# A delta-rule scan whose DRAM tensors are laid out by chunk of 64 tokens, with its small packing transfers joined and its decays loaded in halves

## The chip, the cores and the metric

The kernel runs on one core of a Trainium2 chip. A core has five engines that run side by side and meet only at semaphores: TensorE (PE in the rows, with its weight loads as PEld), VectorE (DVE), ScalarE (ACT), GpSimd (POOL) and SyncE (SP). Here SyncE issues every transfer between DRAM and the core's memory (SBUF), in one queue, in the order of its program; 16 DMA engines carry them out. The metric is device time of one execution, in microseconds (us).

## The reference

Everything is float32. The program is one hybrid decoder block; six of its stages touch what is changed here. Cut to what they compute, for H = 16 heads of 128 and T = 2048 tokens:

```
q, k, v = (silu(dwconv_causal(x @ W.T, taps of 4)) for each W in Wq, Wk, Wv); k *= 128 ** -0.5
a    = sigmoid(x @ Wa.T + ba)         # a decay for each head and value dimension
beta = sigmoid(x @ Wb.T + bb)         # one number for each head
def step(St, inp):                    # St is (head, 128, 128), over 2048 tokens
    err = einsum('bhij,bhj->bhi', St, kt) - vt
    Sn  = at[..., None] * St - (bt[..., None] * err)[..., None] * kt[:, :, None, :]
    ot  = einsum('bhij,bhj->bhi', Sn, qt)
out = layernorm_per_head(o) * sigmoid(x @ Wg.T) @ Wo.T + x
```

Behind it stand a feed-forward layer, a sparse attention and a second feed-forward layer; the change leaves them alone.

## The kernel before, in words

The stages run one after another, each with its own buffers and semaphores and a barrier behind it.

**project_phase** computes, head by head, five streams (beta_k, q, k, beta_v and a, the decay) as 128 x 2048 tiles and stores each as one megabyte in DRAM, laid out (head, partition, token): one run of 8 KB on each partition. SyncE stores them in `stores`, and behind them loads the row of beta and the weights of the head after next.

**gram_phase** loads keys, beta_k and q of one head (three transfers of 1 MB, two heads in flight), multiplies keys with themselves and with q in windows of 144 tokens, and stores the products near the diagonal in `band` (8 transfers of 64 KB a head) and the transposed keys in `kT` (8 transfers of 128 KB a head).

**scan_phase** is the recurrence. It goes through 128 blocks of C = 16 tokens, all 16 heads at once. Four blocks (BPC) make a chunk of 64 tokens, two chunks a turn (RING = 128 tokens, 8 blocks); `v` is a block's place in its chunk. Three kinds of work are prepared chunk by chunk: SyncE packs dot products out of `band` into `dots` (`pack_dots`), loads them to all partitions (`load_dots`, 2.5 MB), copies bands into two zero-padded DRAM buffers `xz` and `uz` (`build`, 24 transfers a chunk) and loads those (`load_grams`); ScalarE negates some dots (`negate`, in block v = 0); GpSimd makes out of dots and decays the small triangular matrices of the next chunk (`prepare`, 33 operations and more, a chunk ahead).

In each block VectorE runs four steps (`solve(0)` to `solve(3)`). Each but the last hands its result to TensorE to be turned (L1519), ScalarE copies it (L1402), TensorE applies it to the rest of the block (L1529), and the next `solve` begins with L1677. Among these steps VectorE multiplies the four quarters of the state by the block's decays, `decay_state(0)` in the middle of the block, (1) later, (2) and (3) at its end (L1733). Before the first quarter it waits for `abar`, the decays of this block spread to all partitions, 1 MB in one buffer:

```
dve.wait_ge(abar_in, 16 * (b + 1))          # decay_state(0)
sp.wait_ge(s_decayed, 4 * (b + 1))          # SyncE: all four quarters done,
load_abar(b + 1)                            # then the next block's decays
```

SyncE's queue in a chunk, in order: v = 0 loads keys and grams of the next chunk and abar; v = 1 packs the dots of a chunk of the next turn (28 transfers) and loads abar; v = 2 builds (24 transfers) and loads abar; v = 3 loads k and q, abar, then, once GpSimd has finished `prepare` (`pre_done`), the decays `avec` and the dots `gram` for GpSimd's next chunk, and v. The stores of the output stand in v = 1 and v = 3. `avec` and `gram` have one buffer each.

Two operations of VectorE in a block take both of their inputs from SBUF: `carry_first` (L1700, in the first third of a block) and the scaling of UB (L1750, in its middle). GpSimd's `prepare` works in SBUF alone.

**mix_phase** loads the scan's output `o` head by head (L547, 64 transfers of 256 KB), norms and gates it and multiplies by Wo.

## Time and profile before

| | us |
|---|---|
| median of 3 runs | 9192.23 (9132.13 to 9202.69) |
| the profiled execution | 9095.78, span 9094.0 |
| projections | 207 to 1072 |
| gram stage | 1120 to 1415 |
| scan, from the first to the last decay of a state quarter | 1504.3 to 4344.2 |
| mix stage | 4388 to 4975 |

The span is the time from the first to the last instruction of the profiled execution. That execution is one run; the median above is of three others and lies 1.05% higher. A group of rows below is one answer of the trace. "Idle before" is the time in which an engine stood still before an instruction, with the instruction or transfer that released it. SPq is SyncE's queue: the duration of a row there is that of issuing, not of the transfer.

### The profile page before, as it was taken

The page shows a single profiled execution, that of the slowest core. Times are in us where ns is not written, and L with a number is a line of the kernel's source. Part 1 is how long each engine was busy: PE and PEld are TensorE (multiplying, and loading weights), DVE is VectorE, ACT ScalarE, POOL GpSimd, SP SyncE. Part 2 cuts the span into 40 slices and gives each one's busy share as a digit, 9 for nine tenths or more (in the row PEclk, how much of TensorE's full clock was granted, in tenths as well). Part 3 has the DMA queues.
Part 4 walks back from the last instruction along what each step waited for, and adds up shares of the span by engine and source line. Part 5 has one row for each costly group of instructions (what it writes and reads, how often), then busy time and mean ns, then how long its engine had stood idle before and what let it go on. Part 6 is the DMA issues. An engine that isn't in the chain of part 4 may idle for free. (4 is left out here: it accounts for less than half of the span.)

```text
span 9094.0 us, 86277 instructions
## 1 busy us (share of the span) xinstructions
PE 6326.3 (70%) x24276; PEld 3976.1 (44%) x24276; DVE 5051.7 (56%) x7260; ACT 2599.2 (29%) x4821; POOL 2080.9 (23%) x1465
## 2 busy tenths in 40 slices
PE   2888663555555555565697996955435989989799
PEld 1766542333333333333354784422224842222487
DVE  3888712656756666666566332277887743333332
ACT  1322221232223223232343211144431223333121
POOL 0554404445454535453010110100000000000011
PEclk6999875555555555555799997966555568888899
DMA  4333485545454444444212003211102211110200
GB/s 145 135 136 130 153 261 139 154 124 147 115 156 137 136 138 136 140 132 123 100 55 68 28 21 113 78 45 35 28 15 45 56 42 38 28 37 20 101 28 26
DMA packets 960301, 850.70 MB, mean 94 GB/s; under 512 B 656944, under 2 KB 834736, under 8 KB 907952
## 3 DMA queue, kind: packets, MB, share of 16 engines
q1 hardware_dynamic: 960032, 847.89, 31.9%
q14 instruction: 195, 1.60, 0.1%
q8 instruction: 74, 1.21, 0.1%
HBM read 655.85 MB, written 198.63 MB: 94 GB/s over the span
## 5 line engine op out<-in xcount | busy, mean ns | idle before, releaser
L888 POOL TENSOR_TENSOR ffn_hid_low<-ffn_hid,ffn_hid_high 128x512 fp32r<-128x512 f32 x128 | 164.9, 1288 | 3581.3 <-ACT ffn_hid_high L878 3581.3
L298 PE MATMUL proj_acc<-proj_xn,proj_w 128*128 128x512 f32 x3072 | 729.1, 400 | 125.0 <-ACT proj_decay L344 90.8
L1529 PE MATMUL scan_pq<-scan_inner,scan_uT 64*128 64x128 f32 (+1 forms) x768 | 341.9, 545 | 599.2 <-ACT scan_uT L1402 416.5
L2351 PE MATMUL attend_ot<-attend_e,attend_v 128*64 128x512 f32 (+3 forms) x1280 | 693.4, 632 | 90.2 <-ACT attend_e L2378 90.2
L298 PEld LDWEIGHTS proj_acc<-proj_xn,proj_w 128*128 128x128 f32 x3072 | 594.3, 194 | 259.8 <-ACT proj_decay L344 93.8
L391 DVE SCALAR_TENSOR_TENSOR proj_y<-proj_raw,proj_cw,proj_y 128x2048 f32<-128x2048 f32 x144 | 574.5, 3990 | 19.1 <-DVE proj_y L387 2.7
L1519 PE MATMUL scan_turn<-scan_idt,scan_ud 128*128 128x128 f32 x384 | 172.2, 449 | 573.9 <-DVE scan_ud L1689 552.2
L1975 PE MATMUL csum_sc<-csum_qk 96*128 96x512 f32 (+3 forms) x640 | 289.6, 569 | 395.6 <-ACT csum_e L1999 350.2
L1733 DVE TENSOR_TENSOR scan_S<-scan_S,scan_abar 128x512 f32<-128x512 f32 x508 | 339.3, 691 | 313.6 <-DMA scan_abar<-decays 313.3
L1529 PEld LDWEIGHTS scan_pq<-scan_inner,scan_uT 64*128 64x128 f32 (+1 forms) x768 | 182.7, 295 | 717.0 <-ACT scan_uT L1402 509.3
L1677 DVE TENSOR_TENSOR scan_pq<-scan_pq,scan_reach 128x48 f32<-128x48 f32 x512 | 108.8, 212 | 688.7 <-PE scan_pq L1529 624.3
L941 DVE TENSOR_TENSOR ffn_hid<-ffn_gate,ffn_l 128x512 f32<-128x512 f32 x128 | 88.0, 687 | 583.0 <-PE ffn_l L824 352.2
L2019 DVE TENSOR_REDUCE csum_mx<-csum_sc 128x1 f32<-128x2048 f32 (+15 forms) x256 | 327.4, 1284 | 143.9 <-PE csum_sc L1978 143.9
L2410 DVE SCALAR_TENSOR_TENSOR attend_sc<-attend_far,attend_hcol,attend_sc 128x128 f32<-128x128 f32 x464 | 141.4, 348 | 474.4 <-PE attend_sc L2340 382.2
L2236 DVE TENSOR_REDUCE cmax_peak<-cmax_sc 128x1664 f32 (+22 forms) x256 | 328.1, 1291 | 116.1 <-PE cmax_sc L2197 113.8
L1519 PEld LDWEIGHTS scan_turn<-scan_idt,scan_ud 128*128 128x128 f32 x384 | 67.1, 175 | 739.9 <-DVE scan_ud L1689 433.3
L1483 PE MATMUL scan_S<-scan_UTm,scan_kT 32*128 32x256 f32 x2032 | 385.0, 675 | 0.0
L824 PE MATMUL ffn_g<-ffn_xn,ffn_w 128*128 128x512 f32 x1536 | 372.6, 392 | 10.4 <-issue 10.4
L824 PE MATMUL ffn_l<-ffn_xn,ffn_w 128*128 128x512 f32 x1536 | 369.0, 389 | 0.0
L1975 PEld LDWEIGHTS csum_sc<-csum_qk 96*128 96x128 f32 x640 | 156.9, 279 | 482.1 <-ACT csum_e L1999 408.0
L2340 PEld LDWEIGHTS attend_sc<-attend_qk 98*128 98x128 f32 x640 | 132.7, 207 | 525.4 <-issue 284.3
L2378 ACT ACTIVATE attend_e<-attend_sc,attend_hcol 128x512 f32<-128x512 f32 (+3 forms) x448 | 271.2, 605 | 258.7 <-PE attend_sc L2340 256.5
(230 smaller groups left out, 14390.7 us busy)
## 6 DMA issues: line engine op xcount, KB each, us to landing
scan_abar<-decays SPq DMA_DIRECT2D x128, 1024.0 KB, 5.2
scan_gram<-dots SPq DMA_DIRECT2D x32, 2560.0 KB, 13.4
scan_cross<-xz SPq DMA_DIRECT2D x128, 256.0 KB, 5.0
scan_inner<-uz SPq DMA_DIRECT2D x32, 1024.0 KB, 7.5
csum_qk<-qk SPq DMA_DIRECT2D x96, 256.0 KB
cmax_qk<-qk SPq DMA_DIRECT2D x96, 256.0 KB
attend_qk<-qk SPq DMA_DIRECT2D x96, 256.0 KB
proj_beta_rows<-beta SPq DMA_DIRECT2D x16, 1024.0 KB, 8.2
```

The source lines that it names most:

```text
L298: mm = pe.matmul(acc[:, (j * TT + t) % 8, :], w[:, u, wh, j, k, :], xn[:, xh, k, t * TOK:(t + 1) * TOK], start=(p == 0 and k == 0), stop=( ...
L391: dve.scalar_tensor_tensor(y[:, s % 2, :], src, cwt, y[:, s % 2, :], ALU.mult, ALU.add).then_inc(conv_step, 1)
L824: mm = pe.matmul(ps[:, x % 2, :], w[:, u, wh, k, n * P:(n + 1) * P], xn[:, xh, k, t * TOK:(t + 1) * TOK], start=(a == 0 and k == 0), stop= ...
L1483: mm = pe.matmul(S[:, q, g].rearrange("p e i -> p (e i)"), keys[32 * q:32 * q + 32, g, :], UTm[32 * q:32 * q + 32, g].rearrange("p e i -> ...
L1519: pe.transpose(turn_ps[:, 0:P], ud[:, slot:slot + 2].rearrange("p j h s -> p (j h s)"), idt[:, :]).then_inc(ut_done, 1)
L1529: pe.matmul(pq[:, u % 2].rearrange("p h w t -> p (h w) t")[:, :, t0:t0 + n], uT[0:k, :], inner[0:k, half, v, :, t1:t2], start=False, stop= ...
L1733: dve.tensor_tensor(S[:, q], S[:, q], abar[:, q], ALU.mult).then_inc(s_decayed, 1)
L1975: pe.matmul(sc[:, n % 2, c:c + w], qk[:, u, 0, q * P:(q + 1) * P], qk[:, u, 1, c:c + w], start=True, stop=(c + w < (q + 1) * P))
L2019: dve.tensor_reduce(mx[:, n % 2:n % 2 + 1], sc[:, n % 2, 0:(q + 1) * P], AX.X, ALU.max, negate=True).then_inc(maxed, 1)
L2236: dve.tensor_reduce(peak[:, bass.ds(h * NT + q, 1)], sc[:, n % 2, 0:(q + 1) * P], AX.X, ALU.max, negate=True).then_inc(peaked, 1)
L2351: pe.matmul(ot[:, g % 2, lo:TOK], v[:, u, kt, :], e[:, x % RINGS, lo:TOK], start=(kt == 0), stop=(x == last_of[g])).then_inc(summed, 1)
L2378: op = act.activation(e[:, x % RINGS, near:TOK], sc[:, x % RINGS, near:TOK], ACT.Exp, bias=hcol[:, u, kt:kt + 1], scale=SCALE)
```

## The change

The streams, the transposed keys, the padded buffers and the output are laid out in DRAM so that what the scan loads for a chunk lies in one run on each partition: streams as (chunk, partition, head, 64 tokens), `kT` as (chunk, half, partition, 4 blocks x 128), `xz` and `uz` with the four blocks of a chunk side by side, `o` as (32 tokens, partition, head, 32). What writes the streams (projections) and what reads them head by head (gram stage, mix stage) now moves pieces: 256 bytes each for the streams, 128 bytes for `o`.

The rows of `band` are shifted by their block's place in the chunk (row length ROW = 112 instead of 64), so that the 16 units of a chunk lie at even distances: `pack_dots` needs 7 transfers of 256 pieces instead of 28 of 64. `abar` is loaded in two halves with a semaphore each; the first half is asked for once two quarters of the state are done. `build` is cut by block and spread over v = 1 (one), v = 2 (two), v = 3 (one). `avec` and `gram` are loaded at v = 2 instead of v = 3. In the prologue the packing stands ahead of the loads of k and q.

```diff
-    streams = [scratch(f"stream_{n}", (H, P, T)) ...]
+    streams = [scratch(f"stream_{n}", (T // CHUNK, P, H, CHUNK)) ...]
-    band = scratch("band", (H, GH, C, T // P, 2, 2 * C))
-    kT = scratch("kT", (2 * T // C, P, P))
-    xz = scratch("xz", (2, BPC, 2, P * 256 + 256))
-    uz = scratch("uz", (2, BPC, P, 512))
+    band = scratch("band", (H, GH, C, T // P, ROW))
+    kT = scratch("kT", (T // CHUNK, 2, P, BPC * P))
+    xz = scratch("xz", (2, 2, P * BPC * 2 * GH * C + GH * 2 * C))
+    uz = scratch("uz", (2, P, BPC * 2 * H * C))
-    o = scratch("o", (H, P, T))
+    o = scratch("o", (T // (2 * C), P, H, 2 * C))
...
             def pack_dots(it, half):
-                for v in range(BPC):
-                    at0 = band[:, BPC * half + v, 0, bass.ds(it, 1), 0]
-                    for q, row in ((1, 0), (1, 1), (1, 2), (1, 3), (0, 0), (0, 1), (0, 2)):
...
-                        rows = bass.AP(band.tensor, at0.offset + row * TROW + q * C + first, [[HROW, H], [4 * TROW + 4, 4], [1, n]])
+                at0 = band[:, BPC * half, 0, bass.ds(it, 1), 0]
+                for q, row in ((1, 0), (1, 1), (1, 2), (1, 3), (0, 0), (0, 1), (0, 2)):
...
+                    rows = bass.AP(band.tensor, at0.offset + row * TROW + q * C + first, [[HROW, H], [4 * TROW + 4, SPC], [1, n]])
...
-            def load_abar(b):
-                sp.dma_start(abar[:, :, :, :, :]..., decays[bass.ds(b, 1), :].to_broadcast([P, H * P])).then_inc(abar_in, 16)
+            def load_abar(b, part):
+                sp.dma_start(abar[:, 2 * part:2 * part + 2]..., decays[..., part * H * P // 2:(part + 1) * H * P // 2]...).then_inc(abar_in[part], 16)
...
-                    if u % BPC == 2 and more:
-                        sp.wait_ge(grams_in[half], 16 * 5 * (it + 1))
-                        build(it + 1, half)
+                    if v == 1 and more:
+                        sp.wait_ge(grams_in[half], 16 * 2 * (it + 1))
+                        build(it + 1, half, 0)
+                    if v == 2 and more:
+                        build(it + 1, half, 1)
+                        build(it + 1, half, 2)
+                    if v == 3 and more:
+                        build(it + 1, half, 3)
                     if more or u < BPR - 1:
+                        sp.wait_ge(s_decayed, 4 * b + 2)
+                        load_abar(b + 1, 0)
                         sp.wait_ge(s_decayed, 4 * (b + 1))
-                        load_abar(b + 1)
-                    if u % BPC == BPC - 1 and more:
+                        load_abar(b + 1, 1)
+                    if v == 2 and more:
                         sp.wait_ge(pre_done, 2 * it + half + 2)
                         load_a(it + 1, half)
                         load_dots(it + 1, half)
...
                 def decay_state(q):
-                    if q == 0:
-                        dve.wait_ge(abar_in, 16 * (b + 1))
+                    if q % 2 == 0:
+                        dve.wait_ge(abar_in[q // 2], 16 * (b + 1))
```

How SyncE's queue moves, in two places. The names are target<-source, then the shape; a row that ends in x2 stands for two such transfers.

SyncE, end of block v = 2 and block v = 3 in the first turn, before:

```order
L1296 DMA scan_abar<-decays 128x2048
L1234 DMA scan_ring<-stream_beta_k 128x16x64
L1234 DMA scan_ring<-stream_q 128x16x64
L1296 DMA scan_abar<-decays 128x2048
L1243 DMA scan_avec<-stream_a 128x16x64
L1261 DMA scan_gram<-dots 128x5120
L1292 DMA o<-scan_oring 128x16x32
```

and with the change:

```order
L1300 DMA scan_abar<-decays 128x1024 x2
L1251 DMA scan_avec<-stream_a 128x1024
L1267 DMA scan_gram<-dots 128x5120
L1244 DMA scan_ring<-stream_beta_k 128x1024
L1244 DMA scan_ring<-stream_q 128x1024
L1273 DMA xz<-band 16x16x32
L1277 DMA uz<-band 16x4x12
L1279 DMA uz<-band 16x4x4
L1277 DMA uz<-band 16x4x12
L1279 DMA uz<-band 16x4x4
L1281 DMA uz<-band 16x4x32
L1300 DMA scan_abar<-decays 128x1024 x2
```

`avec` and `gram` stood behind the second abar of this stretch, at the end of block v = 3, and now stand behind the abar of v = 2, a block earlier; six transfers of a build lie between k, q and the next abar.

SyncE, block v = 1 in the first turn, with the change, from the abar ahead of it on (before, the same place had 28 rows `dots<-band 16x4x4` to `16x4x1` and no build):

```order
L1300 DMA scan_abar<-decays 128x1024 x2
L1263 DMA dots<-band 256x1x4
L1263 DMA dots<-band 256x1x3
L1263 DMA dots<-band 256x1x2
L1263 DMA dots<-band 256x1x1
L1263 DMA dots<-band 256x1x3
L1263 DMA dots<-band 256x1x2
L1263 DMA dots<-band 256x1x1
L1273 DMA xz<-band 16x16x32
L1277 DMA uz<-band 16x4x12
L1279 DMA uz<-band 16x4x4
L1277 DMA uz<-band 16x4x12
```

The packing is 7 transfers with 256 rows each where it was 28 with 64; one build of six transfers follows, of which four show here, and then the two halves of abar.

## Rows read from the trace of the kernel before

**Rows 1.** Stages: stretch, us, busy of PE, PEld, DVE, ACT, POOL; clock, DMA share, GB/s.

```profile
207.00:1072.00 865.00, 729.05 (x3072) 594.31 (x3072) 731.00 (x237) 252.13 (x319) 432.99 (x107) 0.93 0.37 132
1120.00:1415.00 295.00, 190.86 (x768) 145.64 (x768) 58.58 (x128) 86.29 (x192) 0.00 (x0) 0.79 0.88 261
1504.30:4344.20 2839.90, 1598.57 (x8491) 945.54 (x8493) 1819.65 (x4052) 830.55 (x1766) 1300.07 (x1085) 0.54 0.48 135
4388.00:4975.00 587.00, 520.19 (x1536) 294.37 (x1536) 358.61 (x272) 234.93 (x247) 66.64 (x64) 0.95 0.18 58
```

**Rows 2.** Waits in the scan, 1440 to 4370: us in total, times, longest us.

```profile
DVE scan_pq L1677 <- PE scan_pq L1529: 624.3, 305, 33.7
...
ACT scan_gram L1361 <- DMA scan_gram<-dots: 398.1, 32, 49.7
...
DVE scan_S L1733 <- DMA scan_abar<-decays: 313.3, 65, 8.8
```

**Rows 3.** SyncE in order of time over one chunk: start us, us to issue.

```profile
2627.88 21.27 SPq L1257 DMA_DIRECT2D dots<-band  x28
2649.42 0.36 SPq L1296 DMA_DIRECT2D scan_abar<-decays  x1
...
2663.25 0.55 SPq L1268 DMA_DIRECT2D xz<-band  x1
...
2672.59 0.36 SPq L1296 DMA_DIRECT2D scan_abar<-decays  x1
...
2673.68 4.21 SPq L1234 DMA_DIRECT2D scan_ring<-stream_q  x1
...
2688.61 4.04 SPq L1261 DMA_DIRECT2D scan_gram<-dots  x1
```

**Rows 4.** VectorE in order of time over the same chunk; in brackets the idle time.

```profile
2655.06 0.70 DVE L1733 TENSOR_TENSOR scan_S<-scan_S,scan_abar 128x512 f32<-128x512 f32 x1 [6.36 <-DMA scan_abar<-decays]
...
2678.05 0.70 DVE L1733 TENSOR_TENSOR scan_S<-scan_S,scan_abar 128x512 f32<-128x512 f32 x1 [8.82 <-DMA scan_abar<-decays]
...
2705.07 0.22 DVE L1677 TENSOR_TENSOR scan_pq<-scan_pq,scan_reach 128x48 f32<-128x48 f32 x1 [11.28 <-PE scan_pq L1529]
...
2711.15 1.49 DVE L1722 TENSOR_REDUCE scan_oring<-scan_oprod 128x256 f32<-128x1280 f32 x1
...
2719.53 0.69 DVE L1733 TENSOR_TENSOR scan_S<-scan_S,scan_abar 128x512 f32<-128x512 f32 x1
...
2724.38 0.69 DVE L1733 TENSOR_TENSOR scan_S<-scan_S,scan_abar 128x512 f32<-128x512 f32 x1
...
2728.36 1.49 DVE L1722 TENSOR_REDUCE scan_oring<-scan_oprod 128x256 f32<-128x1280 f32 x1
```

**Rows 5.** The start of the scan, GpSimd and VectorE in order of time.

```profile
1465.02 1.80 POOL L1559 TENSOR_TENSOR scan_gram<-scan_avec,scan_gram 128x512 f32<-128x512 f32 x1 [15.44 <-ACT scan_gram L1361]
...
1538.68 0.22 DVE L1677 TENSOR_TENSOR scan_pq<-scan_pq,scan_reach 128x48 f32<-128x48 f32 x1 [33.67 <-PE scan_pq L1529]
```

**Rows 6.** VectorE beside GpSimd: one stretch, then groups (busy us, mean ns, idle).

```profile
2084.63 15.66 DVE L1750 TENSOR_TENSOR scan_UB<-scan_ud,scan_suffix 128x192 f32<-128x192 f32 x1
...
2085.24 2.99 POOL L1562 TENSOR_TENSOR scan_Mhat<-scan_Mhat,scan_gram 128x768 f32<-128x768 f32 x1
...
2099.11 0.97 POOL L1562 TENSOR_TENSOR scan_Mhat<-scan_Mhat,scan_tmp 128x256 f32<-128x256 f32 x1
...
L1750 DVE TENSOR_TENSOR scan_UB<-scan_ud,scan_suffix 128x192 f32<-128x192 f32 x127 | 192.8, 1518 | 0.0
...
L1700 DVE TENSOR_TENSOR scan_ud<-scan_ud,scan_reach 128x64 f32<-128x64 f32 x128 | 111.5, 871 | 0.0
```

**Rows 7.** Columns of rows 1: 8 KB pieces loading (gram stage), 256-byte pieces (scan).

```profile
1154.00:1158.00 4.00, 0.00 (x0) 0.00 (x0) 0.00 (x0) 0.00 (x0) 0.00 (x0) 0.50 1.02 406
2678.00:2681.00 3.00, 0.51 (x2) 0.24 (x2) 2.85 (x9) 0.28 (x1) 0.00 (x0) 0.50 1.25 223
```

**Rows 8.** Waits of ScalarE in the projections, 207 to 1072.

```profile
ACT proj_w L310 <- DMA proj_ab<-in_ba: 48.9, 14, 4.7
```

More of the change, by code:

```diff
@@ L960 @@
 DOTS = 20
+ROW = 4 * C + CHUNK - C
 def gram_phase(nc, streams, band, kT_dram, padded, ident, T):
@@ L995, in load @@
             def load(h, u):
-                one = lambda s: streams[s][bass.ds(h, 1)].rearrange("o p t -> p (o t)")
-                sp.dma_start(keys[:, u, :], one(KK)).then_inc(k_in[u], 16)
-                sp.dma_start(both[:, u, 0, 0:T], one(KB)).then_inc(both_in[u], 16)
-                sp.dma_start(both[:, u, 1, 0:T], one(QQ)).then_inc(both_in[u], 16)
+                one = lambda s: streams[s][:, :, bass.ds(h, 1)].rearrange("c p o t -> p c (o t)")
+                pieces = lambda x: x.rearrange("p (c t) -> p c t", t=CHUNK)
+                sp.dma_start(pieces(keys[:, u, :]), one(KK)).then_inc(k_in[u], 16)
+                sp.dma_start(pieces(both[:, u, 0, 0:T]), one(KB)).then_inc(both_in[u], 16)
+                sp.dma_start(pieces(both[:, u, 1, 0:T]), one(QQ)).then_inc(both_in[u], 16)
             def store(i, u):
@@ L1243, in load_a @@
                 sp.dma_start(avec[:, :, :, :].rearrange("p h n s -> p h (n s)"),
-                             streams[3][:, :, bass.ds(it * RING + half * CHUNK, CHUNK)]
-                             .rearrange("h p t -> p h t")).then_inc(a_in, 16)
+                             streams[3][bass.ds(2 * it + half, 1)].rearrange("o p h t -> p (o h) t")).then_inc(a_in, 16)
             def pack_dots(it, half):
-                for v in range(BPC):
-                    at0 = band[:, BPC * half + v, 0, bass.ds(it, 1), 0]
-                    for q, row in ((1, 0), (1, 1), (1, 2), (1, 3), (0, 0), (0, 1), (0, 2)):
-                        first = row + 1 - q
-                        n = 4 - first
-                        place = 4 * row if q else 13 + 3 * row
-                        rows = bass.AP(band.tensor, at0.offset + row * TROW + q * C + first, [[HROW, H], [4 * TROW + 4, 4], [1, n]])
-                        out = bass.AP(dots.tensor, half * DOTS * U + (4 * v) * DOTS + place, [[SPC * DOTS, H], [DOTS, 4], [1, n]])
-                        sp.dma_start(out, rows, allow_slow_non_contiguous=n == 1).then_inc(packed[half], 16)
+                at0 = band[:, BPC * half, 0, bass.ds(it, 1), 0]
@@ new lines, in pack_dots @@
+                for q, row in ((1, 0), (1, 1), (1, 2), (1, 3), (0, 0), (0, 1), (0, 2)):
+                    first = row + 1 - q
+                    n = 4 - first
+                    place = 4 * row if q else 13 + 3 * row
+                    rows = bass.AP(band.tensor, at0.offset + row * TROW + q * C + first, [[HROW, H], [4 * TROW + 4, SPC], [1, n]])
+                    out = bass.AP(dots.tensor, half * DOTS * U + place, [[SPC * DOTS, H], [DOTS, SPC], [1, n]])
+                    sp.dma_start(out, rows, allow_slow_non_contiguous=n == 1).then_inc(packed[half], 16)
@@ L1298, in _ @@
             load_a(0, 0)
-            load_kq(0, 0)
             pack_dots(0, 0)
             load_dots(0, 0)
-            build(0, 0)
+            load_kq(0, 0)
+            for v in range(BPC):
+                build(0, 0, v)
             load_keys(0, 0)
@@ L1305, in _ @@
             load(RV, 0, 0, vb_in[0])
-            load_abar(0)
+            for part in range(2):
+                load_abar(0, part)
             load_kq(0, 1)
@@ L1309, in _ @@
             pack_dots(0, 1)
-            build(0, 1)
+            for v in range(BPC):
+                build(0, 1, v)
             sp.wait_ge(pre_done, 1)
@@ L1344, in turn @@
                         store(it, u)
-                    if u % BPC == BPC - 1:
-                        if more:
-                            sp.wait_ge(r_done, NSUB * (b + 1))
-                            load(RV, it + 1, half, vb_in[half])
+                    if v == BPC - 1 and more:
+                        sp.wait_ge(r_done, NSUB * (b + 1))
+                        load(RV, it + 1, half, vb_in[half])
             turn(0, True)
```

107 lines of the change are left out of this document (55 added, 52 removed).

## The prediction

> **What bounds the kernel.** I read first the busy time by stage [rows 1]. The change touches four stages. In the scan, 2840 us for 127 blocks or 22.4 us a block, no engine is full: VectorE is busy 64%, TensorE 56% at a granted clock of 0.54 of full, near the lower of its two levels (1.2 of 2.4 GHz), the DMA engines 48%. So the scan is a chain of short steps through VectorE, TensorE and ScalarE, and what counts is what holds that chain. The gram stage is the opposite: the DMA engines are busy 88% at 261 GB/s. In the projections VectorE leads (85%) and DMA has room (37%); in the mix stage TensorE leads and DMA is at 18%.
>
> Then the waits of the scan [rows 2]. VectorE waits 313.3 us for `abar` in 65 places, and 624.3 us before L1677, for the step that TensorE and ScalarE give back. Most of the latter is the chain itself; the part that can go is that ScalarE waits 398.1 us for the dots `gram` before `negate`, and the copy that VectorE needs next stands behind it in ScalarE's program.
>
> Then one chunk in order of time [rows 3, 4]. Packing takes SyncE 21.27 us, building the 23.2 us from 2649.42 to 2672.59, and each has an abar behind it that could have gone earlier; VectorE stands 6.36 and 8.82 us. `avec` and `gram` go out at the very end of the chunk, and in the next block VectorE stands 11.28 us. That is 26.5 us of 89.5 a chunk. A block with none of this, from one reduction of the output to the next, takes 17.2 us (2711.15 to 2728.36).
>
> Last, VectorE beside GpSimd [rows 6]. The two operations with both inputs in SBUF are sometimes held: L1750 took 15.66 us, until GpSimd's run of instructions was over (2099.11 + 0.97). Against the 0.35 and 0.22 us that they take unheld, they lose 127 x 1.17 + 128 x 0.65 = 232 us, 7.5 us a chunk. The change leaves GpSimd's work as it is.
>
> **The sum**, against the profiled execution (9095.8 us).
>
> *The waits for abar.* Seven packing transfers take, at the 0.74 us from one small transfer to the next (a piece-rich one of 256 rows, xz, issues in 0.55 us too [rows 3]), about 5.3 us, and the build between them 4.5. In the clean block the first quarter is decayed 8.4 us and the second, done, 13.9 us after the reduction before [rows 4]. So the first half of abar may be asked for 5.5 us after its last use, and 17.2 - 5.5 = 11.7 us before the next, where the whole went out at the block's end, about 6 before. SyncE's longest piece of work, 10 us at v = 1, starts at the block's end and is over before the next half may go. All 313 us go: **-313**. The cover for what stays of packing and build is that slack; without it each late us would be a us again.
>
> *The wait for gram.* It is asked for a block earlier, when `prepare` has ended. GpSimd's last operation waits for ScalarE at the end of v = 2, so this comes about 1 us into v = 3, and 2.6 MB need some 12 us to land, ahead of the next chunk by 4 or more. ScalarE's wait without the start is (398.1 - 49.7 - 15) / 30 = 11.1 us; VectorE's 11.28 less the usual 1.6 is 9.7. I take 9.8 for 30 chunks: **-295**. Late next is GpSimd, which may start only when the chunk is over, and has about 43 us of work for 70: it holds nobody.
>
> *The start* [rows 5]. GpSimd waits 15.44 us for dots packed by 28 transfers; with 7, and with k and q behind, they come 18 us sooner: -15. The second gram goes out behind two packings, and VectorE stands 33.67 us; it will go out once the first `prepare` is over, and 2.6 MB then leave some 14: -20. **-35**.
>
> *What comes back.* While VectorE stood for abar, TensorE finished the step that it waits for next, and no idle time follows. Without the stall the usual 1.5 us are there again, 65 times: **+100** (bounds 0 and 100).
>
> *The holds.* `prepare` now starts with the chunk, not with gram's arrival, and its unbroken run then lies from 18.7 to 41.4 us in the chunk. The L1700 of block v = 1 (at 19.9) falls just inside, where it lay just ahead; the others lie as before. I take 1.6 us a chunk: **+50**. Bounds: no holds at all, -232; each chunk held as rival B has it, +255.
>
> The scan: -493, that is 18.5 us a block; the clean one above plus the mean holds (7.5 + 1.6 a chunk) would be 19.5, so the -493 leans on blocks without a meeting of the two engines.
>
> *The gram stage.* Its loads become 4096 pieces of 256 bytes a MB. The same size of piece, from the same streams, ran at 223 GB/s in the scan with the DMA engines full, and 8 KB pieces at 406 [rows 7]: 4.7 us a MB against 2.6. The window of small pieces begins with the tail of an abar and is short, so I take 1.9 of the 2.1 us, 3 loads, 16 heads: **+90**, as DMA bounds the stage. Bounds: +45, if only the two-deep wait from load to product grows; +150, if the stores behind are held as well.
>
> That row is where a rule can be weighed: it shows 1.8 times the time for small pieces. The Trainium skill (DMA: Bandwidth & Descriptors, Why small descriptors are slow (HBM only)) gives a 256-byte descriptor 11 cycles where its data need 8, 3/8 more. By that rule, an estimate, the loads would cost 1.0 us more each, the stage +48, the total 8763 instead of 8805. I go by the row.
>
> *The projections.* Five stores a head in small pieces, 2 us more each, 160 us of DMA in 865 that are 37% full: hidden. But the weights stand behind two of these stores, 4 us later, and ScalarE already waits 3.5 us for them, 14 times [rows 8]. ScalarE has room (252 of 865 us); I take a quarter: **+15** (0 to +60). *The mix stage.* Loads of 128-byte pieces, with four buffers and DMA at 18% [rows 1]: **0** (to +5).
>
> The sum is -493 + 90 + 15 = **-388**: 8708 for the profiled execution, 1.05% below the median shown; from the median **9192 - 388 = 8804, taken as 8805 us**.
>
> **The rivals.**
>
> *B: holds in each chunk, at L1750.* GpSimd's start now hangs on VectorE's own reduction, so the phase between them repeats, and may repeat badly: 15.7 us, 31 times, is 487 instead of 232 + 50. +205: **9010**. For it: one such hold is there [rows 6]; against: before, too, phases nearly repeated and the mean was 7.5.
>
> *C, slower than before: held at L1700 of v = 1.* The same place, one operation earlier, to the end of GpSimd's run: 22.7 us in each chunk, 704 instead of 282. +422: **9227**, and more with the gram stage at its bound. It decides when more than 29 of 31 chunks are so held ((387 + 282) / 22.7). For it: the operation now falls inside the run; against: most operations that meet GpSimd lose under 1 us.
>
> For both, the row shows a hold across many GpSimd instructions, the longest 2.99 us. The Trainium skill (SBUF — State Buffer, SBUF: two separate sides) has a lock on a shared port pair held for the full instruction, whoever starts first. By it a hold ends with one instruction, B and C fall away, and the -232 bound would nearly be met in both kernels; the row speaks against it.
>
> *D: small pieces are bound by their number.* The load of q is held 4.21 us at issue behind 2048 pieces [rows 3]; at 2.06 ns a piece a MB takes 8.4 us, the gram stage +278 instead of +90, and the projections, five stores a head and weights 12 us late, about +100 more: **9090**. Against it: the same two loads were through at 223 GB/s [rows 7], half that time.
>
> *E: the change does not do what it says.* If 256 tiny pieces take SyncE as long as four times 64, packing keeps its 21 us; with a build behind it the first half of abar is 6 us late once a chunk (31 x 6 = 186), and the start gains nothing (+35): **9025**. Against it: the 0.55 us of xz.
>
> **The numbers.** Forecast 0.70, B 0.12, C 0.05, D 0.07, E 0.06. Low end: the forecast with half the holds gone, nothing back and the gram stage at +45, 8805 - 205 = 8600. High end: B with the gram stage near its upper bound, 9060; this takes in E and leaves out C, D and the tails, under 2 in 10. The forecast alone spans 8620 to 8950. 1% (92 us) is about what a measurement can tell from no change. Faster by more: forecast, B, E and half of D, less a little for tails, 0.87. Within 1%: half of D and most of C, 0.08. Slower: 0.05.
>
> **What would show it.** No wait of L1733 for abar above a few us in total; ScalarE's wait for gram down to the start; packing under 6 us in SyncE's order of time; the scan at 2300 to 2400 us; L1750 and L1700 at a mean near 1.6 and 1.0 us (B: 4 us for L1750; C: 6 us for L1700); the gram stage at 370 to 400 us; loads of keys landing 2 us a MB later. I am wrong if the scan stays above 2600, if the holds exceed 15 us a chunk, or if projections grow by more than 60 us.

## The result and the profile after

| | before | changed |
|---|---|---|
| median of 4 runs, same chip | 9186.24 us (9132.13 to 9202.69) | 8901.78 us (8854.96 to 9053.65) |
| ratio of the runs | | 0.9676, 95% interval 0.9622 to 0.9730 |
| the profiled execution | 9095.78, span 9094.0 | 9053.65, span 9051.9 |

The change is faster by 284 us, 3.1% by the medians; 8805 us was forecast, with 8600 to 9060 around it. The profiled execution of the change is the longest of its runs; it is read first, and a second one of 8945.17 us (experiment e0_again) beside it. The ratios leave out slow executions, those more than 1.5% above the fastest of their kernel in a series: the 9053.65 us (granted clock 0.716 where the others have 0.720 to 0.724), 4 of the 10 of e4_streams, 1 of the 14 of before beside e1_psum to e4_streams, and 5 of the 7 of before beside e0_again, e5_heads, e6_both and e7_before_psum, so that the ratios of these four rest on two executions of before (9108.90 and 9180.51 us).

The four stages of [rows 1] in the profile of the change (stretch, us, busy time of PE, PEld, DVE, ACT, POOL; granted clock, DMA share, GB/s):

```profile
206.40:1057.10 850.70, 729.68 (x3072) 594.33 (x3072) 719.34 (x233) 247.71 (x313) 437.45 (x106) 0.92 0.57 133
1134.90:1523.60 388.70, 190.65 (x764) 145.07 (x765) 58.10 (x127) 85.19 (x191) 0.00 (x0) 0.71 0.99 192
1600.10:4309.70 2709.60, 1596.61 (x8491) 942.60 (x8493) 2240.85 (x4052) 826.00 (x1766) 1293.97 (x1085) 0.53 0.41 141
4367.00:4935.50 568.50, 516.18 (x1526) 291.55 (x1524) 356.16 (x268) 234.88 (x247) 66.54 (x64) 0.96 0.25 51
```

The gram stage takes 388.7 us instead of 287.3 (first to last of its matmuls), with DMA full at 192 GB/s instead of 261. The scan takes 2709.6 instead of 2839.9, 130 us less where 493 were forecast. The odd number is VectorE's: with the same 4052 operations it is busy 2240.85 us instead of 1819.65. Projections and mix stage are where they were.

The waits of [rows 2] in the same stretch, 1440 to 4370 (us in total, times, longest):

```profile
DVE scan_pq L1691 <- PE scan_pq L1543: 381.3, 328, 10.5
...
ACT scan_gram L1375 <- DMA scan_gram<-dots: 60.5, 2, 31.5
...
SPq L1300 <- DVE scan_S L1747: 1691.3, 253, 25.5
...
POOL scan_pair L1573 <- DVE scan_oring L1736: 462.4, 30, 15.7
```

L1691 is L1677 of before, L1747 is L1733, L1300 issues abar. No wait for abar is left, and ScalarE's for the dots only at the start; SyncE now waits for VectorE. The last row is new: GpSimd starts each chunk's `prepare` when VectorE has reduced the output of a chunk, where it used to start when avec had landed.

SyncE in order of time over a chunk, as in [rows 3] (start us, us to issue):

```profile
2613.80 0.33 SPq L1251 DMA_DIRECT2D scan_avec<-stream_a  x1
2614.19 0.42 SPq L1267 DMA_DIRECT2D scan_gram<-dots  x1
...
2649.29 5.01 SPq L1263 DMA_DIRECT2D dots<-band  x7
```

Packing takes 5.01 us instead of 21.27. So packing, abar and gram did what was forecast. Then VectorE's groups of [rows 6] under their new lines (busy us, mean ns), and a stretch of VectorE and of GpSimd:

```profile
L1714 DVE TENSOR_TENSOR scan_ud<-scan_ud,scan_reach 128x64 f32<-128x64 f32 x128 | 507.3, 3963 | 0.0
...
L1764 DVE TENSOR_TENSOR scan_UB<-scan_ud,scan_suffix 128x192 f32<-128x192 f32 x127 | 220.6, 1737 | 0.0
```

```profile
2650.36 21.52 DVE L1714 TENSOR_TENSOR scan_ud<-scan_ud,scan_reach 128x64 f32<-128x64 f32 x1
...
2698.74 1.49 DVE L1736 TENSOR_REDUCE scan_oring<-scan_oprod 128x256 f32<-128x1280 f32 x1
...
2715.43 1.49 DVE L1736 TENSOR_REDUCE scan_oring<-scan_oprod 128x256 f32<-128x1280 f32 x1
```

```profile
2649.51 2.35 POOL L1573 TENSOR_TENSOR scan_gram<-scan_avec,scan_gram 128x768 f32<-128x768 f32 x1
...
2670.80 1.00 POOL L1576 TENSOR_TENSOR scan_Mhat<-scan_Mhat,scan_tmp 128x256 f32<-128x256 f32 x1
```

carry_first (L1714) began 0.85 us after GpSimd's run of 14 operations and ended with it, 21.52 us later instead of 0.22. The two operations take 727.9 us together, against 304.3 before: 21 times carry_first was held for 21.5 to 23.1 us, 10 times the scaling of UB (L1764) for 15.6 to 16.7, that is once in each of the 31 chunks (before: one of 23.1 and 9 of 15.4 to 16.7). A block without a hold takes 16.7 us (2698.74 to 2715.43), less than the 17.2 of before.

Not every meeting of the two engines ends so. VectorE, then GpSimd beside it, twice in this profile, when carry_first began 0.23 us into the last operation ahead of the run of 14:

```profile
2392.10 23.06 DVE L1714 TENSOR_TENSOR scan_ud<-scan_ud,scan_reach 128x64 f32<-128x64 f32 x1
...
3081.86 0.84 DVE L1714 TENSOR_TENSOR scan_ud<-scan_ud,scan_reach 128x64 f32<-128x64 f32 x1
```

```profile
2391.87 0.99 POOL L1576 TENSOR_TENSOR scan_That<-scan_That,scan_tmp 128x256 f32<-128x256 f32 x1
...
3081.63 0.99 POOL L1576 TENSOR_TENSOR scan_That<-scan_That,scan_tmp 128x256 f32<-128x256 f32 x1
```

The first was held to the end of the run, the second only to the end of the one operation that it met. And in the kernel before, 0.49 us into an operation inside the run, as the 15.66 us of [rows 6] were (2084.63, with GpSimd's operation from 2084.14):

```profile
2180.37 0.87 DVE L1750 TENSOR_TENSOR scan_UB<-scan_ud,scan_suffix 128x192 f32<-128x192 f32 x1
```

```profile
2179.88 1.15 POOL L1559 TENSOR_TENSOR scan_Mhat<-scan_That,scan_gram 128x256 f32<-128x256 f32 x1
```

Counted over the scan, for each of the two operations of VectorE that began while GpSimd was in the last operation ahead of the run or in one of the run's 14:

| met by VectorE | kernel, profile | held to the end of the run | let in after one operation |
|---|---|---|---|
| the operation ahead of the run | before | 1 | 30 |
| | changed, 9053.65 | 7 | 10 |
| | changed, 8945.17 | 4 | 13 |
| an operation of the run | before | 14 | 36 (and 1 after two) |
| | changed, 9053.65 | 24 | 0 |
| | changed, 8945.17 | 24 | 11 |

What decides between the two no run here shows.

This splits every scan in two numbers: these two operations, and all the rest (first to last quarter of the state, less the two operations).

| scan of | us | the two operations | the rest |
|---|---|---|---|
| before | 2839.2 | 304.3 | 2534.9 |
| changed, profile of 9053.65 | 2709.0 | 727.9 | 1981.1 |
| changed, profile of 8945.17 (e0_again) | 2619.7 | 636.5 | 1983.2 |

(Stretches from the start of the first quarter to the start of the last row of quarters, which holds two, so 0.6 us shorter than in the stages above.) The rest fell by 554 us in the one and 552 in the other; the two profiles of the changed kernel differ by 89.3 us in the scan and by 91.4 in the two operations.

### The profile page after: what moved, and what is told of

The parts are those of the page before. It is cut to its first block and busy times, and to the rows that moved or that the text cites. A ratio compares the mean times of both kernels' runs of the same rounds, so it can differ in the third digit from the quotient of the medians.

```text
span 9051.9 us, 84901 instructions
## 1 busy us (share of the span) xinstructions
PE 6324.7 (70%) x24276; PEld 3975.8 (44%) x24276; DVE 5473.4 (60%) x7260; ACT 2594.1 (29%) x4821; POOL 2083.0 (23%) x1465
## 5 line engine op out<-in xcount | busy, mean ns | idle before, releaser
L1714 DVE TENSOR_TENSOR scan_ud<-scan_ud,scan_reach 128x64 f32<-128x64 f32 x128 | 507.3, 3963 | 0.0
L1416 ACT ACTIVATE scan_uT<-scan_turn 128x128 f32<-128x128 f32 x384 | 107.4, 280 | 981.9 <-PE scan_turn L1533 981.9
L1691 DVE TENSOR_TENSOR scan_pq<-scan_pq,scan_reach 128x48 f32<-128x48 f32 x512 | 109.4, 214 | 433.8 <-PE scan_pq L1543 381.3
```

What stands on the lines that cost most here:

```text
L1714: dve.tensor_tensor(ud[:, 0], ud[:, 3], reach[:, half, :, 4 * v + 1, 3].unsqueeze(2).to_broadcast([P, H, 4]), ALU.mult).then_inc(u_carried, 1)
```

## The experiments

My theory after the profile of 9053.65 us, before e0_again was run: the forecast of the waits held, and what was missing of the gain is held time of VectorE beside GpSimd. The rivals: the holds only cover waits that would stand there anyway; any small operation is slow at that time; the profile of 9053.65 us was slow for some other reason.

### e1_psum: one input of the held operations out of PSUM

```
+ dve.tensor_reduce(carry_ps, reach[:, half, :, 4 * v + 1, 3:4], AX.X, ALU.add)        # one input each,
+ dve.tensor_reduce(scales_ps, suffix[:, half, :, v, :].unsqueeze(3), AX.X, ALU.add)   # result in PSUM
- dve.tensor_tensor(ud[:, 0], ud[:, 3], reach[:, half, :, 4 * v + 1, 3]..., ALU.mult)
+ dve.tensor_tensor(ud[:, 0], ud[:, 3], carry_ps..., ALU.mult)
- dve.tensor_tensor(UB..., ud[:, 0:3]..., suffix[:, half, :, v, :]..., ALU.mult)
+ dve.tensor_tensor(UB..., ud[:, 0:3]..., scales_ps..., ALU.mult)
```

> The changed kernel, but the two VectorE operations of a block that take both inputs from SBUF (in carry_first and at the scaling of UB) take one input from PSUM: two small one-input VectorE operations ahead of carry_first copy the 16 ends and the 48 scales into the idle half of a PSUM buffer. Theory A (a two-input operation out of SBUF is held while GpSimd's unbroken run lasts, in each of the 31 chunks: 21 holds of about 22 us at carry_first, 10 of about 15.6 at the scaling of UB in the profile of the change): both operations take under 2 us in every block, about 620 us of held time goes, two operations of some 0.2 to 0.5 us are added to a block (30 to 60 us in all), and the scan from first to last quarter falls from 2709.6 us in the profile of the change to 2130 to 2250: a total of 8350 to 8500. Theory B (the holds cover time that VectorE would wait for TensorE or SyncE anyway): the holds go, but waits take their place, and the total stays above 8750. Theory C (what is held is any small VectorE operation at that time, whatever its operands): the new copies are held instead, for the same 15 to 23 us, and the total stays at 8850 to 8950.

Measured: 8452.13 us, 0.9274 of before (0.9233 to 0.9314); in the scan 2114.9 us. VectorE's rows, groups first, then in the middle of GpSimd's run, and GpSimd's beside them:

```profile
L1773 DVE TENSOR_TENSOR scan_UB<-scan_ud,scan_pq 128x192 f32<-128x192 f32 x127 | 44.9, 354 | 0.0
...
L1722 DVE TENSOR_TENSOR scan_ud<-scan_ud,scan_pq 128x64 f32<-128x64 f32 x128 | 28.3, 221 | 0.0
L1719 DVE TENSOR_REDUCE scan_pq<-scan_suffix 128x48 f32<-128x48 f32 x128 | 26.3, 205 | 0.0
L1718 DVE TENSOR_REDUCE scan_pq<-scan_reach 128x16 f32<-128x16 f32 x128 | 23.2, 181 | 0.0
...
2696.22 0.35 DVE L1773 TENSOR_TENSOR scan_UB<-scan_ud,scan_pq 128x192 f32<-128x192 f32 x1
...
2705.54 0.22 DVE L1722 TENSOR_TENSOR scan_ud<-scan_ud,scan_pq 128x64 f32<-128x64 f32 x1
```

```profile
2695.75 1.18 POOL L1574 TENSOR_TENSOR scan_Mhat<-scan_That,scan_gram 128x256 f32<-128x256 f32 x1
...
2705.38 2.51 POOL L1577 TENSOR_TENSOR scan_Mhat<-scan_Mhat,scan_tmp 128x512 f32<-128x512 f32 x2
```

Both operations, and the two copies, take their unheld time in all blocks, inside GpSimd's run too: 122.7 us for the four groups. The rest of the scan is 2114.9 - 122.7 = 1992.2 us, 9 to 11 more than in the changed kernel. So all of the held time was on the path, nothing took its place, and it hangs on having both inputs in SBUF. Theory A holds; its total was met (its scan, 2130 to 2250, lay a little above the 2114.9), B and C fall.

### e2_gaps: gaps in GpSimd's run

```
+ pool.wait_ge(t_ready, c + 1)          # and pre_step, pre + 20 to pre + 33:
  ...                                   # each of 14 operations waits for the one before
```

> The changed kernel, but GpSimd waits for the end of its own previous operation ahead of each of the 14 operations of its long unbroken run in prepare, so that the run has gaps; nothing else is altered. Theory A (a held operation of VectorE gets in at the first gap of GpSimd's run): no hold lasts over 4 us, against 21.5 to 23.1 and 15.6 to 16.7 us in the profile of the change, and the total falls by 300 to 550, to 8350 to 8600. Theory B (the hold lasts as long as GpSimd has work on shared operands, gaps or none): holds stay at 15 to 25 us and the time stays within 60 of the change's, or grows by the waits.

Measured: 8482.86 us, 0.9302 (0.9263 to 0.9340), scan 2158.7, the two operations 183.1 and the rest 1975.6. The longest such operation takes 2.94 us; one of the longest, VectorE, then GpSimd:

```profile
2716.74 2.92 DVE L1779 TENSOR_TENSOR scan_UB<-scan_ud,scan_suffix 128x192 f32<-128x192 f32 x1
```

```profile
2716.49 2.96 POOL L1576 TENSOR_TENSOR scan_Mhat<-scan_Mhat,scan_gram 128x768 f32<-128x768 f32 x1
2719.53 2.07 POOL L1573 TENSOR_TENSOR scan_Mhat<-scan_gram 128x512 f32<-128x512 f32 x1
```

The scaling of UB (L1779 here) begins 0.25 us into a GpSimd operation and is let in when that one ends; the gap is 0.08 us long (2716.49 + 2.96 to 2719.53). None of the 94 meetings from the operation ahead of the run on is held past the operation that it met. The work of GpSimd and the inputs are those of the changed kernel, so no hold over several operations is left once there are gaps. That a missing gap is enough for a long hold is not shown: where VectorE was let in after one operation of the unaltered run, GpSimd's rows have no gap either. Theory A holds. The Trainium skill (SBUF — State Buffer, SBUF: two separate sides) has a VectorE operation with two SBUF inputs locked out for a whole GpSimd instruction that reads SBUF. This run agrees with it to the instruction (2.92 us, to the end of one), and so do the short meetings of the table above; the long ones do not, where the hold lasted over 14 instructions (21.52 us).

### e3_shift: GpSimd starts later

```
+ pool.wait_ge(r_done, 4 * free + 3)    # ahead of prepare: three steps of block v = 0
```

> The changed kernel, but GpSimd begins the next chunk's prepare later in block v = 0: only when VectorE has three of the four steps of that block behind it, some 7 us later. Theory A (which of the two operations is held, and for how long, is a matter of where GpSimd's unbroken run of about 23 us begins in the block of 16.7 us): carry_first of block v = 1 is now ahead of the run and is held in fewer than 10 chunks; the holds move to the scaling of UB in v = 1 (some 15 to 20 us) or to carry_first of v = 2 (some 6 to 12 us), and the sum over the kernel changes from about 650 us to between 350 and 600; the time falls by 0 to 250. Theory B (carry_first of v = 1 is slow for another reason, such as a wait for TensorE's results in PSUM): its 21 long instances stay where they are, and the time stays within 40.

Measured: 8800.39 us, 0.9647 (0.9603 to 0.9691). VectorE, then GpSimd's run, then SyncE's packing, which is issued in v = 1:

```profile
2740.28 15.88 DVE L1715 TENSOR_TENSOR scan_ud<-scan_ud,scan_reach 128x64 f32<-128x64 f32 x1
```

```profile
2733.73 2.30 POOL L1573 TENSOR_TENSOR scan_gram<-scan_avec,scan_gram 128x768 f32<-128x768 f32 x1
...
2755.13 0.95 POOL L1576 TENSOR_TENSOR scan_Mhat<-scan_Mhat,scan_tmp 128x256 f32<-128x256 f32 x1
```

```profile
2723.85 5.01 SPq L1263 DMA_DIRECT2D dots<-band  x7
```

The held carry_first starts 16.4 us behind the packing, so it is now that of v = 2; in the changed kernel it started 1.1 us behind (2650.36 and 2649.29). 26 chunks are so held, for 13.6 to 15.9 us; only one scaling of UB is held long. The two operations take 502.9 us, the rest 1965.8. Theory A met in place and in sum; the hold in v = 2 is 14 to 16 us long, not 6 to 12, since the run reaches further into that block than I had reckoned (to 2756.08).

### e0_again: the changed kernel once more

No edit.

> The changed kernel again, with a new profile. Its profile of 9053.65 us was 1.7% above the median of its runs, with carry_first held in 21 chunks for about 22 us and the scaling of UB in 10 for 15.6. Theory A (the holds depend on where GpSimd's run falls in a block, and that varies from execution to execution): a profile near 8860 to 8910 shows the same gram stage and the same unheld blocks of 16.7 us, but 150 to 200 us less in the two held operations, about 450 to 500 in place of 656. Theory B (such an execution is quicker by its clock or its transfers): the held time is again 620 to 690 us, and the unheld block is shorter, about 15.5 us.

Measured: 8997.28 us (8945.17 to 9016.57), 0.9830 (0.9728 to 0.9932), by which alone it would be unclear whether the gain exceeds 2% on this chip. In the profile, 14 holds of carry_first of 21.5 to 23.1 us, 13 of the scaling of UB of 15.6 to 16.7, and 4 chunks with short ones alone: 636.5 us against 727.9, with the rest equal within 2.1 us (table above). The held time, that is the 636.5 without the 73 that the two operations take unheld, is 564 us where it was 655; a block without a hold takes 16.7 us as before, and the gram stage is the same within 1 us. Theory A in its mechanism: 91 of the 108 us between the two profiles are held time. In size neither was met, since this execution was not as fast as I had assumed (A said 450 to 500, B 620 to 690).

### e4_streams: the streams' layout alone, in the kernel before

```
- streams = [scratch(..., (H, P, T)) ...]
+ streams = [scratch(..., (T // CHUNK, P, H, CHUNK)) ...]    # and its stores and loads
```

> The kernel before, with one part of the change: the five streams lie in DRAM by chunk of 64 tokens (stores of the projections, loads of the gram stage and of the scan follow); keys, Gram tiles, packing and decays are as before. As forecast: the gram stage's 48 loads in pieces of 256 B make it about 90 to 100 us longer (TensorE's gram work takes 287.3 us before, 388.7 in the change), projections stay within 15, the scan gains or loses up to 30: a total of 9230 to 9320. Rival (the gram stage is longer because its stores of keys and Gram tiles changed as well): the stage stays under 320 us, and the total is within 40 of before.

Measured: 9174.91 us (median of 10 runs) against 9123.26; the ratio is 1.0053 (1.0014 to 1.0093), no difference by the measure of 2%. The profile is 9064.8 us against 9095.8. TensorE's wait for q in the gram stage, in the kernel before, in this one, and in the changed one:

```profile
PE gram_g L1047 <- DMA gram_both<-stream_q: 114.5, 15, 17.3
```

```profile
PE gram_g L1048 <- DMA gram_both<-stream_q: 218.4, 15, 24.3
```

```profile
PE gram_g L1050 <- DMA gram_both<-stream_q: 220.0, 15, 23.9
```

The gram stage is 383.5 us, 98 more than before's 285.5 (from the start of its first row of matmuls to that of its last): the streams' loads carry its price, and the new stores of keys and Gram tiles cost nothing there. But the time grew by much less, since the rest of the scan fell from 2534.9 to 2428.4: ScalarE waits 328.4 us for the dots instead of 398.1 and VectorE 279.7 for abar instead of 313.3, together 103 us. I had expected at most 30 from that side, and a total of 9230 to 9320. So the forecast is met in the gram stage, where the rival falls (383.5, not under 320), and missed in the total.

### e5_heads and e6_both: the streams by head again

The reverse edit, in the changed kernel and in e1_psum.

> The changed kernel, but the five streams lie in DRAM by head again, as before the change, with the gram stage's loads in pieces of 8 KB and the scan's in pieces of 256 B; keys, Gram tiles, packing, halves and the earlier loads are kept. As forecast: the gram stage's matmuls go from 387 us back to 285 to 290, projections stay, and the scan loses at most 30: the time is 70 to 105 us under the changed kernel's. Rival (the scan gained from the streams' layout, since with that part alone it took 2722.2 us from first to last quarter against 2839.2 in the kernel before): the scan grows by 100 to 130 and the time is within 30 of the changed kernel's.

> The changed kernel with two edits: the two held operations of VectorE take one input from PSUM, and the streams lie by head again. If the two effects are independent and the streams' layout costs what the gram stage shows: a scan of 2115 to 2150 us and a gram stage of 285 to 290, in all 8340 to 8370, against 8452 with the first edit alone. Rival (the streams' layout gains in the scan what it loses in the gram stage): 8430 to 8480.

Measured: e5_heads 8894.05 us, 103 less than e0_again on the same chip; the gram stage is 288.2 us instead of 386.5 and the rest of the scan 2023.4 instead of 1983.2. The two profiles differ by 56 us (8889.4 and 8945.2), about what these two parts make (-98 and +40); that the medians differ by 103 they do not explain. e6_both 8369.56 us, 0.9153 of before (0.9090 to 0.9217), with the gram stage at 285.8 and the scan at 2144.3 against 2114.9 in e1_psum. With the queue free, the streams by chunk are worth 29 to 40 us in the scan and cost 98 to 103 in the gram stage; 26.9 us of the former are waits for abar, which come back in e6_both (18 of them, the longest 3.5 us).

Both forecasts are met and both rivals fall. e6_both is the fastest kernel of this study: 628 us (7%) under the changed kernel on the same chip (8997.28).

### e7_before_psum: no holds in the kernel before

The edit of e1_psum in the kernel before.

> The kernel before, but the two VectorE operations of a block that take both inputs from SBUF take one from PSUM, by way of two small copies ahead of carry_first; nothing of the change is in it. Theory A (the holds hid behind waits in the kernel before, and the waits for decays and dots are what bounds it): its 304 us of the two operations fall to about 75, but VectorE and ScalarE meet the waits for decays and for dots in their place, and the time falls by 0 to 100, to 9020 to 9120 against a before of 9123. Theory B (holds and waits add up): it falls by 180 to 240, to 8880 to 8940.

Measured: 8950.46 us, 0.9790 (0.9717 to 0.9864); the profile is 8953.3 against 9095.8. The two operations and the copies take 182 us less (122 for 304.3), and the rest of the scan grew from 2534.9 to 2602, since VectorE meets more waits for abar:

```profile
DVE scan_S L1741 <- DMA scan_abar<-decays: 401.5, 74, 8.7
```

Neither theory is met: 67 of the 182 us came back as waits, by the profiles, not most and not none; the total lies between the two ranges, next to B's. The kernel before had the holds partly covered; the changed one, without waits, has them bare.

### e8_pack28, e9_whole, e10_late: one part of the change undone, without holds

Each is e1_psum (8452.13 us; scan 2114.9) with one edit:

```
e8_pack28:  - 7 transfers, [[HROW, H], [4 * TROW + 4, SPC], [1, n]]
            + for v in range(BPC): 7 transfers, [[HROW, H], [4 * TROW + 4, 4], [1, n]]
e9_whole:   - sp.wait_ge(s_decayed, 4 * b + 2)
              load_abar(b + 1, 0)              # now behind the wait for all four quarters
e10_late:   - if v == 2 and more:              # avec and gram
            + if v == BPC - 1 and more:
```

> The changed kernel with the two held operations on PSUM (8452 us, scan 2114.9 from first to last quarter), but the dots of a chunk are packed by 28 transfers again instead of 7; layouts, halves and earlier loads stay. By the forecast SyncE's queue has about 16 us more in block v = 1 of each chunk (21.3 for 28 transfers before, 5.0 for 7), which is as long as a block: the decays that it issues next come late and VectorE waits for them once a chunk, 5 to 12 us: 150 to 370 us more in the scan. Rival (SyncE has slack: it waits for VectorE 1691 us in the scan of the change, 54 us a chunk, and the decays' first half leaves two quarters earlier): under 60 us more.

> The changed kernel with the two held operations on PSUM, but both halves of a block's decays are issued only after the fourth quarter of the state, as the single load was before the change. By the forecast's term for the halves (decays still land before the next first quarter where nothing else is queued, since a block is 16.7 us and the load lands within 11): VectorE waits for decays in fewer than half of the blocks, by 1 to 3 us: 20 to 120 us more. Rival (the halves carry most of the 313 us of waits that went): over 200 us more.

> The changed kernel with the two held operations on PSUM, but GpSimd's decays and dots of the next chunk but one (avec, gram) are loaded in block v = 3 again, as before the change, and not in v = 2. By the forecast (398.1 us of ScalarE's waits for dots went with this move and the shorter packing): ScalarE waits for the dots again, 5 to 12 us a chunk, in block v = 0 between the copies that the solve steps wait for: 150 to 350 us more. Rival (the dots land in time now, since the queue ahead of them is 16 us shorter and ScalarE reads them only in the next block): under 60 us more.

Measured: 8688.39, 8442.47 and 8673.35 us, all on one chip (0.9343, 0.9071 and 0.9322 of its 9300.42); scans of 2351.0, 2123.4 and 2336.2. e8_pack28, SyncE, then VectorE in the same chunk:

```profile
2676.46 20.97 SPq L1265 DMA_DIRECT2D dots<-band  x28
...
2702.21 0.95 SPq L1302 DMA_DIRECT2D scan_abar<-decays  x2
```

```profile
2706.91 0.70 DVE L1756 TENSOR_TENSOR scan_S<-scan_S,scan_abar 128x512 f32<-128x512 f32 x1 [8.72 <-DMA scan_abar<-decays]
```

The 16 us that packing takes longer push abar's issue past VectorE's need by 8.7 us, once a chunk: 267.8 us of such waits, and a scan 236 us longer. e10_late, SyncE, then VectorE:

```profile
2707.77 0.33 SPq L1252 DMA_DIRECT2D scan_avec<-stream_a  x1
2708.23 0.34 SPq L1268 DMA_DIRECT2D scan_gram<-dots  x1
```

```profile
2722.80 0.22 DVE L1692 TENSOR_TENSOR scan_pq<-scan_pq,scan_reach 128x48 f32<-128x48 f32 x1 [9.33 <-PE scan_pq L1544]
```

ScalarE waits 290.4 us for the dots, VectorE stands 9.33 us in that block, and the scan is 221 us longer. e9_whole waits 0.3 us for abar in the whole scan, whose 8.5 us more are about the difference between two profiles of one kernel. So the earlier load and the shorter packing are worth 221 and 236 us, both as forecast, and asking for half of the decays earlier is worth nothing here, where 20 to 120 us had been forecast: issued after the fourth quarter, both halves still land in time.

### e11_before_halves: the halves alone, from the other end

e7_before_psum with `load_abar(b + 1, 0)` after two quarters and `load_abar(b + 1, 1)` after four.

> The kernel before with the two held operations on PSUM (8950 us; VectorE waits 401.5 us in 74 blocks for decays), and with the decays loaded in halves, the first after two quarters of the state. The first half leaves some 5 us earlier where SyncE's queue is free, but in blocks v = 1 and v = 2 it stands behind 28 and 24 small transfers and gains nothing. Forecast: the wait for decays falls from 401.5 to 150 to 280 us, and the time by 80 to 250. Rival (the waits come from the queue alone, so that the halves are worth nothing without the shorter packing): within 50 of 8950.

Measured: 8891.76 us, on another chip than e7_before_psum; the profile is 8886.8 us of span against 8951.5 in e7_before_psum, scan 2657.3 against 2724.3 (-67). VectorE still waits for abar nearly as long:

```profile
DVE scan_S L1745 <- DMA scan_abar<-decays: 379.2, 63, 9.1
```

The wait for abar fell by 22 us where 120 and more were forecast, and the time by 59, between the forecast's 80 and the rival's 50: where the queue is held by packing and building, half a load earlier does not get past it. A larger part of the 67 us is ScalarE's wait for the dots, 341.4 us instead of 387.0 in e7_before_psum; what made it shorter stays open.

## Why the prediction was right, and which term was off

The sum said -388. Its parts against the profile of 9053.65 us, from stage boundaries and the table above:

| part | forecast | measured |
|---|---|---|
| scan without the two operations, and the stretch ahead of it (abar -313, gram -295, start -35, what comes back +100) | -543 | -554, and -16 ahead |
| the holds | +50 | +424 (+332 in the second profile) |
| gram stage | +90 | +101, and +10 ahead of it |
| projections, mix, what follows | +15 | -8 |

The measured parts give -42, which is 9053.7 against 9095.8; with the second profile it is -151. By the medians the change gained 284 us, and the forecast lay 97 us under the median.

So the time fell inside the range, but by the prediction's own signs it was wrong in the scan: "I am wrong if the scan stays above 2600, if the holds exceed 15 us a chunk", and the two profiles of the change have scans of 2709.6 and 2620 us and holds of 21 and 18 us a chunk. The queue, the loads and the gram stage are foresight. That the total came within 97 us is in part luck: the missing 282 to 374 us of holds show in full between the profiles, whereas by the medians only about 100 us are missing, and of before only an execution 90 us under its median was profiled. What the holds are in an execution near either median no run shows.

- **abar**: right in size. The waits went to none. Of its two reasons one was wrong: e9_whole shows that the halves add nothing where the queue is free, e8_pack28 that the shorter packing is needed. The clean block of [rows 4] could have told: before, abar was asked for only at the block's end, and no wait stood there.
- **gram, start**: right. 60.5 us of ScalarE's waits at the start stay, but the scan starts 16 us earlier and VectorE's longest wait for the step that TensorE gives back (L1677, now L1691) is 10.5 us instead of 33.7. e10_late gives 221 us for the earlier load alone, the two parts overlapping: undone one by one, packing (236), load (221), streams (29) and halves (8) make 494 of the 610 us between the rests of e7_before_psum (2602) and e1_psum (1992). The keys' and padded buffers' layout, the spread of the builds and the order of the prologue were not tested by themselves.
- **What comes back**: close. 643 us of waits and start were taken away, 570 were gained.
- **The gram stage**: right, and by the row that was chosen. 98 to 103 us were measured. The estimate from the Trainium skill's 11 cycles for a 256-byte descriptor (DMA: Bandwidth & Descriptors, Why small descriptors are slow (HBM only)) was 48 us, half of that. Rival D, bound by number of pieces, would have made 278.
- **Streams in the scan**: not in the sum. They are worth 106 us in the kernel before and 29 to 40 in the changed one.
- **Projections**: right that they are hidden; the 15 us were not there.
- **The holds** are the step that failed. "I take 1.6 us a chunk": they grew by 13.7 us a chunk (424 / 31), or 10.7. The place was seen right (carry_first of v = 1 "falls just inside" the run) and the price was wrong: for the 1.6 the prediction names no row, and against rival C it holds that "most operations that meet GpSimd lose under 1 us". Such an operation loses either the rest of one GpSimd operation or the rest of the run, and before it was mostly the former: its carry_first of v = 1 met the operation ahead of the run in all 31 chunks and was let in after it in 30. In the change it was held to the end of the run in 21 of 31 chunks, for 21.5 to 23.1 us, and the scaling of UB, for 15.6 to 16.7, in the other 10 (14 and 13 in the second profile). GpSimd's start now hangs on VectorE's reduction in 30 chunks (462.4 us of waits), but that they meet in every chunk is not new: by the counts above there were 82 such meetings before, 15 of them held to the end of the run, and 41 in the change, 31 of them so held. That the tie between the two engines makes this difference is not shown. That is rivals B and C together, to which the prediction gave 0.12 and 0.05. C, by the profile 8708 + 422 = 9130 us, was not reached, since only 21 of the 31 chunks had the longer hold.

Rival E falls with packing's 5.01 us. Why in one execution 21 chunks and in another 14 fall into the longer hold, and why a meeting at one and the same place ends after one operation or after the whole run, was not settled: e0_again and the first profile are the same program, and the two rows of 23.06 and 0.84 us are of the same execution. Nor was before profiled in one of its longer executions, so what its own spread (9092 to 9391 us in one series) is made of stays open. The kernels without holds spread less: e1_psum 8440 to 8466, e6_both 8363 to 8380 us.

## What to carry to other kernels

When waits are removed around an engine that is sometimes held by another, look at the longest hold and not at the mean: find the other engine's longest run without a gap, and count in how many rounds an operation with both inputs in SBUF can fall into it; and where the earlier holds were short, do not count on their staying so when the meeting moves (here 0.6 us of hold a chunk became 21 to 23 in 21 of 31). Here moving one input to PSUM bought back all 655 us of it for 50 us of copies (two of 0.2 us a block), and a gap in the run bought back 545. A load that is late because of what stands ahead of it in its queue is mended in the queue; cutting it in halves was worth nothing in the changed kernel, and in the kernel before 22 of the 401 us that VectorE waited for it (the scan 67).

## What was not expected of the hardware

- A VectorE operation with both inputs in SBUF, caught in GpSimd's run of 14 operations in SBUF, stood for 21.52 us where it takes 0.22. Others, caught 0.23 us into the operation ahead of that run, stood for 23.06 us or for 0.84, until that one operation was over; with gaps of under 0.1 us between GpSimd's operations all were, and the longest took 2.94 us.
- With one input from PSUM none of the 255 operations of e1_psum took more than 0.36 us; 147 of them began beside an operation of GpSimd, 70 inside the run.
- The quarters of the state, which have one input in PSUM and one in SBUF, took 0.69 us beside GpSimd's run as elsewhere (155 of the 508 of e1_psum began inside it).
- A load in pieces of 256 B takes SyncE longer to issue when it stands behind another such load: in the gram stage of the changed kernel the loads of q took 4.3 us by the median (4.71 in the row below) and those of the keys, the first of a head, 0.64; in that of before, in 8 KB pieces, the loads of q took 0.39:

```profile
1323.30 4.71 SPq L1001 DMA_DIRECT2D gram_both<-stream_q  x1
```

```profile
1317.12 0.40 SPq L999 DMA_DIRECT2D gram_both<-stream_q  x1
```
